# Inner products of a recommendation tower, copied from PSUM with samples innermost instead of columns innermost

## The chip, the core and the metric

The kernel runs on one core of a Trainium2 chip. A core has a matrix engine (TensorE, PE in the profile), three engines for elementwise work (VectorE is DVE, ScalarE is ACT, GpSimd is POOL), a queue engine for DMAs (SyncE, SP), an on-chip memory of 128 partitions (SBUF) and the matrix engine's output memory of 128 partitions by 8 banks of 512 float32 (PSUM). Each engine runs its own instructions in order and waits on semaphores for the others. The metric is the device time of one execution in microseconds, median over the runs shown; lower is better.

## The reference

512 samples, all in float32. Each sample has 26 rows of 64 numbers, looked up in tables, and 256 dense numbers. What is computed:

```python
x = layer_norm(dense_t @ Wd.T, gd, bd)                       # 512 x 128
y = layer_norm(einsum('bnd,ed->bne', sparse_t, Ws), gs, bs)  # 512 x 26 x 128
y = einsum('bne,pn->bep', y, Wsi)                            # 26 rows mixed into 32
y = swapaxes(layer_norm(y, gsi, bsi), 1, 2)                  # 512 x 32 x 128
T = concatenate([x[:, None, :], y], axis=1)                  # 512 x 33 x 128
Z = einsum('bnd,bmd->bnm', T, T)                             # inner products, 33 x 33 a sample
out = layer_norm(Z[:, TRIL_I, TRIL_J] @ Wl.T, gl, bl)        # 528 -> 512, the first 384 used
h = concatenate([out, dense], axis=1)
h = relu(h @ W_top1 + b_top1); h = relu(h @ W_top2 + b_top2); result = h @ W_top3
```

## The kernel before

**Tiles.** The 512 samples are 4 blocks of 128 (`BLOCKS`), a block is 4 units (`BU`), so there are 16 units of 32 samples (`UNITS`), each in two halves of 16. Unit `u` goes through these stages: `transposes` and `norms` on PE, `mult_a`, `sums_a`, `recip_a`, `scale_a` on DVE (the first layer norm, which scales the gathered rows `g_sb` in place), `mix` on PE (`psU`), `keep_u` on ACT (`U`), `project` on PE (`psB`, two halves), `add_b` on DVE (`B`), `squares_b` on ACT (`sqB`), `sums_b` on DVE (`ssB`), `deviation_b` on ACT (`sdB`), `recip_b` and `norm_b` on DVE (`T`), and `inner` on PE: 32 small matmuls, one per sample, the 32 mixed rows against all 33, into `psZ` (seen by the profile as 64 instructions, L333).

**The inner products in PSUM.** `inner(u)` puts the products into four quadrants of 32 partitions, `gq` 0 to 3, eight samples (`GQ`) to a quadrant, and one sample after the other: in a partition there stand 8 samples of 33 columns (`COLS`), 264 numbers without a gap. The last unit uses `psU` in place of `psZ`.

**The copies.** Every quadrant is copied into `Zs` in SBUF, on 32 partitions. There the order is columns first and samples last, 64 samples (`PS`) to a column, so that the neighbour of a number in the next column lies 64 float32 (256 bytes) away and that of the next sample beside it. `z_places(u, gq)` (L206) gives both access patterns. 61 copies are ACT's (`keep_z`, L639) and 3 are DVE's (L1073, for the last two units). `relay` (L212) then moves `Zs` by DMA into `Zt`, on other partitions: 7 DMAs for a block, or for half of the last block. `linear` (L352, L424) multiplies `Zt` by `wl_g`.

**Order.** The order on each engine is written out by hand in a function `step(t)` for every engine. On ACT, step `t` is: `keep_u(t)`, `rows_out(t + 1)` (`sT`), two `squares_b`, `enter_x`, `deviation_a(t + 1)` (`sdA`), then `keep_z(t - 1, 0)`, `deviation_b(t, 0)`, `keep_z(t - 1, 1)`, `keep_z(t - 1, 2)`, `deviation_b(t, 1)`, `keep_z(t - 1, 3)`, and some single instructions of other stages; then `keep_u(t + 1)` of the next step. On DVE it is: two `add_b`, `mult_a` and `sums_a` of the next unit, `sums_b(t, 0)`, `recip_a`, `scale_a`, `sums_b(t, 1)`, then both `recip_b` and `norm_b`. On PE it is: `mix(t)`, `transposes(t + 1)`, `project(t)`, `norms(t + 1)`, `inner(t - 1)` and a part of the linear layers of an earlier block (`linear`, `variance`, `layer1`, `layer2`), or in the first steps other preparation.

**Around the copies.** `inner(u)` waits for the four copies of the unit before (`Z_kept`), since the bank is one. The relays of a block wait for its 16 copies. At the end ACT copies four quadrants in a row and DVE three; when all are there (`Z_kept` 64), the last 7 relays go out on three queues, ACT takes the root of the third block's variance (`zsd`, L660), and the third and fourth block's last layers follow.

Of the kernel before, what the change touches and what calls it, by code (L numbers as in the profile page):

```python
# [13 lines left out]
E, PROJ = 128, 32  # L14
# [6 lines left out]
BLOCKS, BU, HS, US = 4, 4, 64, 16  # L21
# [9 lines left out]
COLS = PROJ + 1  # L31
# [15 lines left out]
GQ = 8  # L47
# [21 lines left out]
def tower(nc, table, ids, small, rows, bs_rows, dense, wl, w1, w2, out):  # L69
    with ExitStack() as ctx:  # L70
        def sb(name, shape, dt=F32):
            return ctx.enter_context(nc.sbuf_tensor(name, shape, dt))
# [74 lines left out]
        Zs = sb("Zs", [PROJ, 2, 2, 7 * CW, PS])  # L147
# [58 lines left out]
        def z_places(u, gq):  # L206
            b, lo = u // BU, 2 * US * (u % 2) + GQ * gq
            bank = psZ if u < UNITS - 1 else psU
            return (Zs[:, b % 2, u % BU // 2, 0:COLS, lo:lo + GQ].rearrange("p c s -> p s c"),
                    bank[gq * PROJ:(gq + 1) * PROJ, 0:GQ * COLS].rearrange("p (s c) -> p s c", s=GQ))  # L210

        def relay(queue, b, q, lo, hi, landed):  # L212

# [367 lines left out]
        def _(act):  # L581
# [48 lines left out]
            def keep_z(u, gq):  # L630
                b, j = u // BU, u % BU
                act.wait_ge(Z_done, 4 * u + gq + 1)
                if j == 0 and gq == 0:
                    if b == 0:
                        act.wait_ge(fills, 5)
                    if b >= 2:
                        act.wait_ge(d_zt[b - 2], 7 * 16)
                to, product = z_places(u, gq)
                act.activation(to, product, ACT.Copy).then_inc(Z_kept, 1)  # L639
# [157 lines left out]
        def _(dve):  # L797
# [272 lines left out]
            for u, gq in ((UNITS - 2, 3), (UNITS - 1, 2), (UNITS - 1, 3)):  # L1070
                dve.wait_ge(Z_done, 4 * u + gq + 1)
                to, product = z_places(u, gq)
                dve.tensor_copy(to, product).then_inc(Z_kept, 1)  # L1073
# [82 lines left out]
```

## Time and profile before

| What | Value |
|---|---|
| median of 3 runs | 186.32 us (186.28 to 187.85) |
| span of the profiled execution | 185.4 us |
| PE busy | 148.0 us (80%) |
| DVE busy | 130.1 us (70%) |
| ACT busy | 106.9 us (58%) |
| POOL busy | 104.3 us (56%) |
| copies of the inner products on ACT (L639) | 61, each about 0.616 us |
| copies of the inner products on DVE (L1073) | 3, each about 0.61 us |

A busy share is an average over the whole span and says nothing of who waits. The order of the steps does: from about 26 us to 164 us the kernel goes through 16 steps of 7 to 10 us, in each of which the four engines hand their work round. What a shorter instruction is worth is read from the wait that ends last in such a step.

### The profile page before, as it was taken

Reading aid. Unit: us, or ns where it says so; the run is one execution under the profiler, and the core shown is the slowest. Engines: PE = TensorE matmul, PEld = TensorE weight load, DVE = VectorE, ACT = ScalarE, POOL = GpSimd, SP = SyncE. Lnnn points to the kernel's source line nnn. Section 1 sums busy time; section 2 is a strip of 40 time slices with the busy share of each in tenths; the row PEclk is TensorE's granted clock in tenths of the full one; section 3 lists DMA queues with packets and bytes.
Section 4 is the critical chain, followed back from the end, with each engine's and each line's share of the span. In section 5 each row is a group of like instructions: output and inputs, shape, how many; then the busy total and the mean of one; then the engine's idle time right before and its main releaser. Section 6 shows DMA issues by size and latency. Waiting matters only on the chain.

```text
span 185.4 us, 4668 instructions
## 1 busy us (share of the span) xinstructions
PE 148.0 (80%) x1825; PEld 113.2 (61%) x1825; DVE 130.1 (70%) x300; ACT 106.9 (58%) x245; POOL 104.3 (56%) x111
## 2 busy tenths in 40 slices
PE   0089877977969947459996978899799799977995
PEld 0084544434549544419794947569596666877994
DVE  6269659772959594908697999579799967943142
ACT  1202435594868486866667877585877857831230
POOL 3778777877878777777777777777840000020000
PEclk9999999996999669855999999999999999997899
DMA  5816334141111112311111123111111100110000
GB/s 153 294 33 194 137 58 161 32 139 26 34 21 29 24 28 61 61 27 27 28 33 23 32 58 64 28 28 25 28 25 40 33 7 11 27 38 0 0 0 0
DMA packets 6003, 9.59 MB, mean 52 GB/s; under 512 B 2303, under 2 KB 3538, under 8 KB 5854
## 3 DMA queue, kind: packets, MB, share of 16 engines
q0 software_dynamic: 3392, 3.45, 10.3%
q1 hardware_dynamic: 2232, 5.08, 9.1%
q10 hardware_dynamic: 358, 0.78, 1.1%
q8 instruction: 14, 0.23, 0.5%
q14 instruction: 7, 0.06, 0.1%
HBM read 8.01 MB, written 0.00 MB: 43 GB/s over the span
## 4 chain that ended last, share of the span: by engine, by line
PE 40%; ACT 23%; DVE 19%; issue 11%; DMA 5%; ACTq 1%; DVEq 0%
PE psB L318 11%; ACT Zs L639 10%; DVE B L831 4%; ACT U L600 4%; DMA dense_sb<-in_dense 4%; PE psG L284 4%; DVE qA L809 4%; DVE prod L802 3%; PE psZ L333 3%; PE psW L352 3%; PE psU L299 3%; DVE ssB L838 3%; ACT sdB L617 2%; PE psB L520 2%; PE psZ L424 2%
## 5 line engine op out<-in xcount | busy, mean ns | idle before, releaser
L257 POOL DMA_INDIRECT g_sb<-in_table,row_id x104 | 102.8, 989 | 31.7 <-issue 31.4
L831 DVE TENSOR_TENSOR B<-psB,bias 128x512 f32<-128x512 f32 x31 | 20.0, 686 | 26.2 <-PE psB L318 26.2
L639 ACT ACTIVATE Zs<-psZ 32x264 f32<-32x264 f32 x59 | 36.3, 616 | 2.1 <-PE psZ L333 1.0
L318 PE MATMUL psB<-U,ws_g 64*128 64x512 f32 x64 | 20.9, 735 | 15.3 <-ACT U L600 15.2
L611 ACT ACTIVATE sqB<-B 128x512 f32<-128x512 f32 x31 | 19.1, 632 | 23.1 <-DVE B L831 23.1
L299 PE MATMUL psU<-wsi_x,g_sb 128*128 128x192 f32 (+4 forms) x128 | 23.3, 330 | 7.3 <-DVE g_sb L824 7.3
L299 PEld LDWEIGHTS psU<-wsi_x,g_sb 128*128 128x128 f32 x128 | 20.9, 206 | 11.1 <-DVE g_sb L824 11.0
L284 PEld LDWEIGHTS psG<-gram,sT 128*128 128x128 f32 x104 | 14.0, 207 | 14.5 <-ACT sT L587 10.0
L850 DVE TENSOR_TENSOR T<-B,rB 128x512 f32<-128x512 f32 x31 | 21.5, 692 | 1.1
L838 DVE TENSOR_REDUCE ssB<-sqB 128x16 f32<-128x512 f32 x32 | 21.7, 677 | 0.1
L284 PE MATMUL psG<-gram,sT 128*128 128x128 f32 x104 | 17.2, 308 | 0.7 <-ACT sT L587 0.7
L318 PEld LDWEIGHTS psB<-U,ws_g 64*128 64x128 f32 x64 | 5.4, 208 | 20.0 <-ACT U L600 20.0
L214 POOL DMA_DIRECT2D Zt<-Zs x2 | 1.1, 549 | 26.5 <-ACT Zs L639 26.5
L333 PE MATMUL psZ<-T 128*32 128x33 f32 x960 | 13.0, 202 | 0.3 <-issue 0.2
L333 PEld LDWEIGHTS psZ<-T 128*32 128x32 f32 x960 | 10.8, 112 | 3.3 <-issue 1.6
L352 PE MATMUL psW<-Zt,wl_g 127*128 127x128 f32 x100 | 12.8, 286 | 0.0
L352 PEld LDWEIGHTS psW<-Zt,wl_g 127*128 127x128 f32 x100 | 12.1, 199 | 0.5 <-issue 0.4
L600 ACT ACTIVATE U<-psU 128x512 f32<-128x512 f32 x16 | 9.5, 595 | 2.5 <-PE psU L299 2.2
L802 DVE TENSOR_TENSOR prod<-psG,g_sb 128x384 f32<-128x384 f32 (+1 forms) x16 | 9.3, 583 | 2.1 <-PE psG L284 2.1
L594 ACT ACTIVATE sdA<-qA,eps_c 128x6 f32<-128x6 f32 (+1 forms) x16 | 4.8, 300 | 9.5 <-DVE qA L812 9.0
L824 DVE TENSOR_TENSOR g_sb<-g_sb,rA 128x384 f32<-128x384 f32 (+1 forms) x16 | 9.5, 592 | 0.6
L809 DVE TENSOR_REDUCE qA<-prod 128x6 f32<-128x384 f32 (+1 forms) x16 | 9.4, 586 | 0.6
(159 smaller groups left out, 226.7 us busy)
## 6 DMA issues: line engine op xcount, KB each, us to landing
g_sb<-in_table,row_id POOLq DMA_INDIRECT x104, 2.5
wl_sb<-in_wl SPq DMA_DIRECT2D x1, 1280.0 KB, 6.0
w_sb<-in_w SPq DMA_DIRECT2D x2, 512.0 KB, 5.4
w_sb<-in_w SPq DMA_DIRECT2D x1, 768.0 KB, 4.5
small_sb<-in_small SPq DMA_DIRECT2D x1, 615.5 KB, 4.1
dense_sb<-in_dense ACTq DMA_DIRECT2D x1, 512.0 KB, 7.3
Zt<-Zs SPq DMA_DIRECT2D x3, 80.0 KB
Zt<-Zs SPq DMA_DIRECT2D x3, 70.0 KB
```

The source lines that it names most:

```text
L257: pool.indirect_dma_start(g_sb[:, k, h * DSP:(h + 1) * DSP], None, table, bass.IndirectOffsetOnAxis(row_id[:, 2 * k + h:2 * k + h + 1], 0) ...
L284: mm = pe.matmul(psG[:, n * P:(n + 1) * P], sT[:, u % 2, n * P:(n + 1) * P], gram[:, :], start=True, stop=True)
L299: mm = pe.matmul(psU[:, (lo - US * j) * PROJ:(hi - US * j) * PROJ], g_sb[:, SLOTS * b + c, :], wsi_x[:, c, lo - s0:hi - s0, :], start=(n = ...
L318: pe.matmul(psB[h][:, :], ws_g[h * DSP:(h + 1) * DSP, :], U[h * DSP:(h + 1) * DSP, u % 2, :], start=not (last and h == 0), stop=True).then ...
L333: mm = pe.matmul(bank[gq * PROJ:(gq + 1) * PROJ, n * COLS:(n + 1) * COLS], T[:, u % 2, h, s, 2:2 + PROJ], T[:, u % 2, h, s, 0:COLS], start ...
L352: mm = pe.matmul(bank[:, at * BS:(at + 1) * BS], wl_g[0:KL, jj, f * P:(f + 1) * P], Zt[0:KL, b, :, jj, :], start=(jj == 0), stop=(jj == CW ...
L600: act.activation(U[:, u % 2, :], psU[:, :], ACT.Copy).then_inc(U_ready, 1)
L611: act.activation(sqB[:, h, :], at, ACT.Square).then_inc(B_squared, 1)
L639: act.activation(to, product, ACT.Copy).then_inc(Z_kept, 1)
L831: dve.tensor_tensor(B[:, h, :].rearrange("p (s j) -> p s j", j=PROJ), psB[h][:, :].rearrange("p (s j) -> p s j", j=PROJ), bias[:, :].rearr ...
L838: dve.tensor_reduce(ssB[:, h, :], sqB[:, h, :].rearrange("p (s j) -> p s j", j=PROJ), AX, ALU.add).then_inc(B_summed, 1)
L850: dve.tensor_tensor(T[:, u % 2, h, :, 2:], at.rearrange("p (s j) -> p s j", j=PROJ), rB[:, h, :].rearrange("p (s o) -> p s o", o=1).broadc ...
```

## The change

One function gives the access patterns of all 64 copies. Before, both were walked with samples outside and columns inside: the read from PSUM was one run of 264 numbers, and the write into `Zs` went 256 bytes on for each number. After, both are walked with columns outside and samples inside: the write goes in runs of 8 numbers side by side (32 bytes), 33 of them, and the read goes 33 float32 (132 bytes) on for each number. The same numbers go to the same places. Nothing else differs: no instruction, wait or buffer is added, removed or moved.

```diff
--- before.py
+++ after.py
@@ -206,8 +206,8 @@
         def z_places(u, gq):
             b, lo = u // BU, 2 * US * (u % 2) + GQ * gq
             bank = psZ if u < UNITS - 1 else psU
-            return (Zs[:, b % 2, u % BU // 2, 0:COLS, lo:lo + GQ].rearrange("p c s -> p s c"),
-                    bank[gq * PROJ:(gq + 1) * PROJ, 0:GQ * COLS].rearrange("p (s c) -> p s c", s=GQ))
+            return (Zs[:, b % 2, u % BU // 2, 0:COLS, lo:lo + GQ],
+                    bank[gq * PROJ:(gq + 1) * PROJ, 0:GQ * COLS].rearrange("p (s c) -> p c s", s=GQ))
```

On ACT the second step with copies reads as follows; each row is a line of the kernel, what it writes and reads, and the shape (partitions, then the free dimensions from the outer to the inner).

```order
 L626 ACTIVATE T<-xT 128x32
 L594 ACTIVATE sdA<-qA,eps_c 128x6
-L639 ACTIVATE Zs<-psZ 32x8x33
-L617 ACTIVATE sdB<-ssB,eps_c 128x16
-L639 ACTIVATE Zs<-psZ 32x8x33 x2
-L617 ACTIVATE sdB<-ssB,eps_c 128x16
-L639 ACTIVATE Zs<-psZ 32x8x33
+L639 ACTIVATE Zs<-psZ 32x33x8
+L617 ACTIVATE sdB<-ssB,eps_c 128x16
+L639 ACTIVATE Zs<-psZ 32x33x8 x2
+L617 ACTIVATE sdB<-ssB,eps_c 128x16
+L639 ACTIVATE Zs<-psZ 32x33x8
 L749 ACTIVATE wl_g,wl_sum<-wl_sb 128x512 x3
```

The places and their neighbours are the same; only the shape of the copies has turned from 8 by 33 to 33 by 8. On DVE the three copies at the end turn in the same way, and PE's rows are the same throughout.

## Rows read from the trace of the kernel before

**Rows 1.** The page: PE's granted clock in 40 slices, and the chain's lines.

```profile
PEclk9999999996999669855999999999999999997899
...
PE psB L318 11%; ACT Zs L639 10%; DVE B L831 4%; ACT U L600 4%; DMA dense_sb<-in_dense 4%; PE psG L284 4%; DVE qA L809 4%; DVE prod L802 3%; PE psZ L333 3%; PE psW L352 3%; PE psU L299 3%; DVE ssB L838 3%; ACT sdB L617 2%; PE psB L520 2%; PE psZ L424 2%
```

**Rows 2.** The waits: engine, line, releaser; us in total, times, longest.

```profile
DVE B L831 <- PE psB L318: 26.2, 15, 4.3
...
ACT U L600 <- PE psU L299: 2.2, 3, 1.7
```

**Rows 3.** ACT by line and shape: count, us busy, mean ns, idle before.

```profile
L639 ACT ACTIVATE Zs<-psZ 32x264 f32<-32x264 f32 x59 | 36.3, 616 | 2.1 <-PE psZ L333 1.0
...
L626 ACT ACTIVATE T<-xT 128x32 f32<-128x32 f32 x16 | 4.0, 248 | 0.0
...
L783 ACT ACTIVATE z_sq<-psZ 128x256 f32<-128x256 f32 x1 | 0.4, 383 | 5.8 <-DVE zT L907 5.8
...
L684 ACT ACTIVATE wsT<-psT 128x128 f32<-128x128 f32 x1 | 0.3, 277 | 1.5 <-PE psT L516 1.5
```

**Rows 4.** DVE by line and shape: copies out of PSUM, and two memsets.

```profile
L1073 DVE COPY Zs<-psU 32x264 f32<-32x264 f32 x2 | 1.2, 612 | 0.1
...
L907 DVE COPY zT<-psZ 128x256 f32<-128x256 f32 x1 | 0.4, 424 | 5.7 <-PE psZ L424 5.7
...
L941 DVE MEMSET gram<- 128x128 f32 x1 | 0.2, 165 | 0.0
...
L938 DVE MEMSET T<- 128x64 f32 x1 | 0.1, 112 | 0.0
```

**Rows 5.** The timeline of step 8, all engines: start, length, engine, line.

```profile
104.00 0.68 DVE L838 TENSOR_REDUCE ssB<-sqB 128x16 f32<-128x512 f32 x1
...
104.33 0.60 ACT L639 ACTIVATE Zs<-psZ 32x264 f32<-32x264 f32 x1
...
104.75 0.28 ACT L617 ACTIVATE sdB<-ssB,eps_c 128x16 f32<-128x16 f32 x1
...
105.05 1.27 ACT L639 ACTIVATE Zs<-psZ 32x264 f32<-32x264 f32 x2
105.29 0.68 DVE L838 TENSOR_REDUCE ssB<-sqB 128x16 f32<-128x512 f32 x1
...
105.79 1.23 PE L299 MATMUL psU<-wsi_x,g_sb 128*128 128x128 f32 x8
...
106.13 0.26 ACT L617 ACTIVATE sdB<-ssB,eps_c 128x16 f32<-128x16 f32 x1
...
106.42 0.63 ACT L639 ACTIVATE Zs<-psZ 32x264 f32<-32x264 f32 x1
...
107.55 0.60 ACT L600 ACTIVATE U<-psU 128x512 f32<-128x512 f32 x1
```

**Rows 6.** The timeline of step 11, ACT and PE.

```profile
129.68 0.61 ACT L639 ACTIVATE Zs<-psZ 32x264 f32<-32x264 f32 x1 [0.28 <-PE psZ L333]
...
130.39 1.26 ACT L639 ACTIVATE Zs<-psZ 32x264 f32<-32x264 f32 x2
...
130.44 1.26 PE L299 MATMUL psU<-wsi_x,g_sb 128*128 128x160 f32 x8
...
132.65 0.59 ACT L600 ACTIVATE U<-psU 128x512 f32<-128x512 f32 x1
```

**Rows 7.** The timeline of ACT where it waits for PE.

```profile
90.04 0.60 ACT L600 ACTIVATE U<-psU 128x512 f32<-128x512 f32 x1 [0.16 <-PE psU L299]
```

**Rows 8.** The timeline where the last copies end.

```profile
162.18 1.25 DVE L1073 COPY Zs<-psU 32x264 f32<-32x264 f32 x2
162.23 1.26 ACT L639 ACTIVATE Zs<-psU 32x264 f32<-32x264 f32 x2
...
163.52 1.73 ACTq L214 DMA_DIRECT2D Zt<-Zs  x2
```

**Rows 9.** The timeline of PE, where it has waited for ACT.

```profile
81.41 2.08 PE L318 MATMUL psB<-U,ws_g 64*128 64x512 f32 x4 [2.12 <-ACT U L600]
```

## The prediction, made before the changed kernel ran

> **What bounds the kernel now.** I read the page first: the chain that ended last changes engines all the time, and no engine is its bound for long. Its second largest line is the one that the change touches, the copies on ACT, with 10% of the span [rows 1]. That is an upper limit, not a price: the chain names what an engine was doing, and something else may be nearly as late. The waits come next: DVE stands 26.2 us for the product `psB`, in 15 waits, while ACT stands only 2.2 us for `psU`, in 3 [rows 2]. So in most of the 16 steps the mixed rows in `psU` are there already when ACT takes them, and ACT is what is late. Last I read the timeline of single steps. A step turns round once from one `U` copy (L600) to the next: `U`, then PE's `psB`, DVE's `B` and its sums, ACT's roots and copies of inner products, and the next `U`.
>
> Step 8 is the common form [rows 5]. DVE's first `ssB` ends at 104.00 + 0.68 = 104.68 and ACT's first root `sdB` starts at 104.75, so it waits for DVE although a copy is in front of it. The second `ssB` ends at 105.29 + 0.68 = 105.97; the second `sdB` starts at 106.13, 0.16 us later. The last copy follows at 106.42, and `U` at 107.55. PE's `mix` had ended at 105.79 + 1.23 = 107.02, so PE would have allowed `U` at about 107.06 (where ACT waits for `mix`, it goes on about 0.04 us after the end).
>
> **What the change does to one copy.** Nothing is added or moved, so the whole matter is the length of 64 instructions. ACT's reads of PSUM that are contiguous and are written contiguously take 277 ns for 128 numbers and 383 for 256 [rows 3]: 106 ns for 128 more, 0.83 ns a number, and 171 ns fixed. The copy of 264 numbers ought to take 171 + 264 x 0.83 = 390 ns. It takes 616, which is (616 - 171) / 264 = 1.69 ns a number, twice as much. The writes that go on by 256 bytes are the only unusual thing in it, since it reads one run. ACT's small write into `T`, with 136 bytes from one number to the next, points the same way: 248 ns for 32 numbers, where the line gives 171 + 27 = 198 (its source is in SBUF, so a part of the 50 ns may be that). DVE shows it too: 612 ns for 264 numbers against 424 for 256 [rows 4]. One pair of rows speaks against it: the memset of 64 places at 136 bytes takes 112 ns, no more for each than the contiguous one of 128 in 165 [rows 4]. A memset reads nothing, so I give it little weight, and a pitch of 136 bytes isn't one of 256.
>
> After the change the write has runs of 8 and should cost what a contiguous one costs. The new cost is the read from PSUM at 132 bytes a number, and no row of this trace has one, on any engine. From below its cost is nothing: 390 ns for a copy on ACT. From above, the nearest row is the strided write itself, 616 ns: the two would then have changed places. A read that is worse than the write is not excluded by any row. I take 390, because what these rows show slow is a write into SBUF, and because a read whose next address is known ahead can be under way while others are finished, which is an argument and no row. That is the choice on which all else hangs.
>
> The Trainium skill ("Advanced Engine Details and Errata", PSUM Cachelines) says the opposite: PSUM works in lines of 8 bytes, so each two consecutive numbers should lie together, and its sentence on patterns with gaps is about matmuls. The same page's SBUF Cachelines (16 bytes, at least two accesses to a line for full rate) agrees with the 616 against 390 ns of the write. By the first rule the gain of the write is lost again in the read and the sum below would be about nothing; this is the second case further down.
>
> **What a step gains.** A copy shortens by 616 - 390 = 0.226 us. That isn't 4 x 0.226 = 0.90 for each of the 14 steps that have four copies, for DVE comes next.
>
> - Common step, by [rows 5]: the copy ahead of the first `sdB` gains nothing, since that root already waits for DVE. The two copies behind it would bring the second root 0.45 earlier, but DVE's `ssB` allows only 105.97 + 0.05 = 106.02, so 0.11. The fourth copy gains its full 0.226. Together 0.33 us, and `mix` allows 107.55 - 107.06 = 0.49, so it stands. Six steps read so (1, 2, 4, 5, 8, 13), with 0.30 to 0.33 each: 1.9 us.
> - Steps with a late first copy, by [rows 6]: in step 11 the copies wait behind `z_sq` and PE's products, until 129.68, when DVE's sums are done. Then all four gain, 0.90, and `mix` (130.44 + 1.26 = 131.70, `U` now at 132.65) allows 0.91. Steps 7, 9 and 11 are like it: 2.7 us.
> - Steps where `mix` is late. `U` at 90.04 waits for PE [rows 7]. Steps 3, 6 and 12 gain nothing, and steps 10 and 14 only up to `mix`, 0.18 and 0.09: 0.3 us.
> - The end, by [rows 8]: ACT's last copies, four without a pause, end at 162.23 + 1.26 = 163.49, and DVE's last two run from 162.18 to 163.43. ACT would gain 0.9. On DVE a contiguous copy of 264 would take 424 + 8 x 1.04 = 432 ns, 0.18 less than 612; its last two cannot start before PE's last products at about 162.1, so they end at about 163.0. The relays start when both are done, at 163.05 instead of 163.52, and ACT's next root stands behind its own two relays: 0.45 us.
>
> The sum is 1.9 + 2.7 + 0.3 + 0.45 = 5.3 us. The profiled execution has a span of 185.4 us, and the median of the runs is 186.3, 0.9 more for what lies around it. Span after: 180.1; time after: **181.0 us**. The 9 us of busy time that are set free on ACT and the 5.3 of the span are thus two numbers: the rest becomes idle time behind DVE's sums and PE's `mix`.
>
> What is late next: DVE's run from `B` to the second `ssB`, without a gap in it, and PE's linear layers ahead of `mix`. The DMA queues see the relays of a block come a little earlier, into stretches in which nobody waits for them.
>
> PE's clock is the uncertain part of this case. It is granted in full in most slices and falls to the lower level around 42 to 46, 60 to 70 and 76 to 87 us [rows 1], and before most of these falls PE had stood idle for some 2 us. At 81.41, behind 2.12 us of waiting for `U`, `psB` takes 2.08 us [rows 9] at the lower level, 1.2 GHz, half of the full 2.4, so about 1 us more. Shorter steps shorten such pauses by 0.3 us. I cost it at nothing, with one or two such losses either way, so this case has a range of its own of 178.5 to 183.
>
> **The other ways.**
>
> 1. The read costs part of it (copy of 450 to 560 ns). As the second root needs only 0.11 us, even a gain of 0.1 us a copy gives 0.2 in six common steps, 0.4 in three long ones and 0.3 in steps 10 and 14 together; with 0.2 at the end that is 2.9, so 183.4, in a band from 182 to 184.5.
> 2. It costs what the write did (the page's rule on 8-byte lines, at the price that [rows 3] show for 264 scattered numbers): each copy still takes 616, no step moves, and the time is **186.3**. For it: symmetry, and the twofold rate looks like one access in two cycles. Against it: it would have to be so in another memory.
> 3. Slower: the read costs more than the write. There is no cover against a longer copy, for it delays every ACT-bound step in full, four times. At three cycles, 2.5 ns a number, a copy takes 171 + 660 = 831 ns, 0.215 more; 0.86 x 12 steps, 0.4 and 0.7 in steps 3 and 6 beyond what ACT now waits, and 0.8 at the end make 12.2: **198.5**. At 2.5 cycles, 720 ns, it is 0.42 in each of 12 steps, 0.3 in the others and 0.4 at the end: 192. It decides against the change from 30 ns more a copy (0.03 x 4 x 14 = 1.7 us) on. For it: the read goes on by a new, odd pitch (33 numbers) each time, and nothing here bounds it. Against it: no row of ACT or DVE shows a number that costs more than about two of the contiguous ones.
> 4. The copies are short but the steps don't follow, since PE's clock falls once or twice more or DVE holds them: 184.5 to 187. The rows of step 11 leave only 0.01 us beside the full gain, so such a limit is near.
>
> **How the numbers follow.** My forecast has 0.57, case 1 0.08, case 2 0.13, case 3 0.17, case 4 0.05. A measurement of this kernel tells about 1%, 1.9 us, from no change. Faster by more than that: the forecast, case 1 and a small part of case 4, 0.66. Within 1%: case 2 and most of case 4, 0.17. Slower: case 3, 0.17. The range goes from 178 (0.04 left out below, where the clock would have to help) to 189 (most of case 3, some 0.15, left out above).
>
> **What the profile after would show.** The copies (L639) at about 390 ns and DVE's at about 430, if the read is free; at 616 and 612 if the costs changed places; above 650 if it is worse. In a common step the second `sdB` starts 0.05 us after the second `ssB` ends, and `U` comes 0.33 us earlier after the `U` before it, not 0.90. The steps 7, 9 and 11 shorten by 0.9. ACT's waits for DVE `ssB` and for PE `psU` grow; the relays of the end start about 0.5 us closer to the end of the last products. The forecast is wrong if the copies are short and the common step gains 0.1 or 0.9, if the clock falls in another place, or at its root if a number read from PSUM 132 bytes on costs more than one beside it.

## The result and the profile after

| | before | after |
|---|---|---|
| median of 5 runs | 186.28 us (185.39 to 187.85) | **177.3 us** (176.97 to 180.81) |
| ratio of the times, with its 95% interval | | **0.956** (0.951 to 0.961) |
| span of the profiled execution | 185.4 us | 179.0 us |
| mean granted TensorE clock in it | 0.936 | 0.943 |
| first `U` to the last relays' issue in it | 25.77 to 163.52 | 25.53 to 158.74 |

The change gave about 9 us in this comparison, where 5.3 were forecast. Here and below, a ratio sets against each other only the runs within 1.5% of a kernel's fastest in the same comparison, while a median takes them all. The profiled execution of after is one of those in which the clock fell most: the other four have spans of 175.2 to 176.1 us, so its steps are to be read against each other, and its span isn't the typical one.

How much of the 9 us is the clock can be bounded by laying runs of equal mean clock side by side, over all comparisons of this document (33 runs of the kernel before, 9 of the changed one). At 0.981 the spans are 180.0, 181.3 and 181.7 us before and 175.2 to 175.9 in four runs after, 5.5 us less on average; at 0.943 to 0.945 they are 183.9 (11 runs) and 179.6 (2 runs) on average, 4.3 less. The median clock is 0.944 before and 0.961 after. So 4.3 to 5.5 us come at an equal clock, near the forecast, and what goes beyond comes with a clock that falls less.

The page of after: the granted clock, the chain by engine and line, and three groups (busy, mean ns, idle before and what ended it). They answer to [rows 1] and [rows 3].

```profile
PEclk9999999997899657956999999999999999999999
...
PE 44%; DVE 25%; ACT 14%; issue 10%; DMA 5%; ACTq 1%; DVEq 0%
PE psB L318 11%; DVE ssB L838 7%; PE psG L284 6%; PE psW L352 5%; ACT U L600 5%; DMA dense_sb<-in_dense 4%; DVE B L831 4%; DVE qA L809 4%; DVE prod L802 3%; PE psU L299 3%; ACT Zs L639 3%; PE psZ L333 2%; DVE g_sb L824 2%; PE psB L520 2%; ACT wl_g L754 2%
...
L639 ACT ACTIVATE Zs<-psZ 32x264 f32<-32x264 f32 x59 | 22.4, 379 | 1.7 <-PE psZ L333 0.6
...
L617 ACT ACTIVATE sdB<-ssB,eps_c 128x16 f32<-128x16 f32 x32 | 9.7, 304 | 4.1 <-DVE ssB L838 4.0
L600 ACT ACTIVATE U<-psU 128x512 f32<-128x512 f32 x16 | 9.5, 595 | 3.0 <-PE psU L299 2.8
```

A copy on ACT takes 379 ns instead of 616. The copies' share of the chain went from 10% to 3%, and `ssB` on DVE, which had 3%, has 7%: what was ACT's is DVE's now. `sdB` waits 4.0 us for `ssB` in all, and the wait for `psU` grew from 2.2 to 2.8.

DVE's copies at the end, by line and shape in the profile after (612 ns in [rows 4]):

```profile
L1073 DVE COPY Zs<-psU 32x264 f32<-32x264 f32 x2 | 0.9, 430 | 0.2
```

Step 8 of after in the timeline (start, length, engine, line), to be laid beside [rows 5]:

```profile
102.23 0.36 ACT L639 ACTIVATE Zs<-psZ 32x264 f32<-32x264 f32 x1
...
102.61 0.31 ACT L617 ACTIVATE sdB<-ssB,eps_c 128x16 f32<-128x16 f32 x1
...
102.94 0.79 ACT L639 ACTIVATE Zs<-psZ 32x264 f32<-32x264 f32 x2
103.19 0.68 DVE L838 TENSOR_REDUCE ssB<-sqB 128x16 f32<-128x512 f32 x1
...
103.69 1.23 PE L299 MATMUL psU<-wsi_x,g_sb 128*128 128x128 f32 x8
...
103.90 0.31 ACT L617 ACTIVATE sdB<-ssB,eps_c 128x16 f32<-128x16 f32 x1 [0.16 <-DVE ssB L838]
104.23 0.39 ACT L639 ACTIVATE Zs<-psZ 32x264 f32<-32x264 f32 x1
...
105.25 0.60 ACT L600 ACTIVATE U<-psU 128x512 f32<-128x512 f32 x1
```

The first root comes 0.38 us behind the first copy's start, before 104.75 - 104.33 = 0.42, though the copy is 0.24 shorter: it waits for DVE, as before. The second root starts at 103.90, DVE's sum having ended at 103.19 + 0.68 = 103.87, with a wait of 0.16 us that wasn't there before. From the first copy to `U` it takes 3.02 us, before 107.55 - 104.33 = 3.22.

Step 11, to be laid beside [rows 6]:

```profile
126.39 0.38 ACT L639 ACTIVATE Zs<-psZ 32x264 f32<-32x264 f32 x1 [0.31 <-PE psZ L333]
...
126.99 0.79 ACT L639 ACTIVATE Zs<-psZ 32x264 f32<-32x264 f32 x2
...
128.68 0.59 ACT L600 ACTIVATE U<-psU 128x512 f32<-128x512 f32 x1
```

From the first copy to `U`: 2.29 us, before 132.65 - 129.68 = 2.97.

**From `U` to `U`, step by step.** All starts are rows of L600 in the two timelines; the last line is from the last `U` to the relays' issue on ACT. For the common steps the prediction has 0.30 to 0.33 each and the sum of 1.9; the column's split of it among them is made afterwards.

| step | before, us | after, us | gain | forecast |
|---|---|---|---|---|
| 1, 2 | 9.38, 10.32 | 9.07, 10.09 | 0.31, 0.23 | 0.33, 0.33 |
| 3 | 8.07 | 7.66 | 0.41 | 0 |
| 4 | 10.23 | 10.46 | -0.23 | 0.30 |
| 5, 6 | 9.95, 9.26 | 9.78, 8.81 | 0.17, 0.45 | 0.31, 0 |
| 7 | 9.71 | 9.17 | 0.54 | 0.90 |
| 8 | 7.80 | 7.61 | 0.19 | 0.33 |
| 9 | 8.38 | 7.53 | 0.85 | 0.90 |
| 10 | 7.50 | 7.34 | 0.16 | 0.18 |
| 11 | 9.22 | 8.56 | 0.66 | 0.90 |
| 12 | 7.40 | 7.41 | -0.01 | 0 |
| 13, 14 | 7.86, 7.49 | 7.55, 7.40 | 0.31, 0.09 | 0.31, 0.09 |
| the end, to the relays | 8.12 | 7.70 | 0.42 | 0.45 |

Together 4.55 us against 5.3. That leaves 6.4 - 4.55 = 1.85 us of the difference of the two spans outside the steps: 0.24 before the first `U`, and 1.6 behind the relays, where nothing was changed. That is the next reading.

The timeline of PE at the end, of before and then of after, with the idle time ahead in brackets:

```profile
168.12 1.18 PE L397 MATMUL psW<-h1T,w_sb 128*128 128x128 f32 x8 [2.30 <-ACT h1T L779]
169.12 2.33 PE L424 MATMUL psZ<-Zt,wl_g 127*128 127x128 f32 x10
171.24 1.68 PE L397 MATMUL psW<-h1T,w_sb 128*128 128x128 f32 x8
172.75 1.28 PE L424 MATMUL psZ<-Zt,wl_g 127*128 127x128 f32 x10
```

```profile
163.34 1.16 PE L397 MATMUL psW<-h1T,w_sb 128*128 128x128 f32 x8 [1.79 <-ACT h1T L779]
164.34 1.28 PE L424 MATMUL psZ<-Zt,wl_g 127*128 127x128 f32 x10
165.46 1.06 PE L397 MATMUL psW<-h1T,w_sb 128*128 128x128 f32 x8
166.35 1.28 PE L424 MATMUL psZ<-Zt,wl_g 127*128 127x128 f32 x10
```

The same ten matmuls take 2.33 us before and 1.28 after, the next eight 1.68 and 1.06. From the first row to the fourth it is 4.63 us before and 3.01 after, which is the whole 1.6. The windows of PE there (us, PE busy and count, granted clock, DMA share, GB/s), before and after:

```profile
170.00:172.00 2.00, 2.00 (x11) 0.50 0.00 0
```

```profile
166.00:168.00 2.00, 2.00 (x20) 1.00 0.00 0
```

The clock stood at the lower level, 1.2 GHz, behind a pause of 2.30 us, and at 2.4 GHz behind one of 1.79. So between these two profiles time was also gained where the change hadn't touched anything, through PE's clock. That the shorter pause is the reason is not shown: in a run further down PE pauses 2.26 us in the same place and keeps the higher level.

### The profile page after: what moved, and what is told of

The parts are those of the page before. It is cut to its first block, busy times and chain, and to the rows that moved or that the text cites. A ratio compares the mean times of both kernels' runs of the same rounds, so it can differ in the third digit from the quotient of the medians.

```text
span 179.0 us, 4668 instructions
## 1 busy us (share of the span) xinstructions
PE 145.6 (81%) x1825; PEld 110.5 (62%) x1825; DVE 129.8 (73%) x300; ACT 98.7 (55%) x245; POOL 103.5 (58%) x111
## 4 chain that ended last, share of the span: by engine, by line
PE 44%; DVE 25%; ACT 14%; issue 10%; DMA 5%; ACTq 1%; DVEq 0%
PE psB L318 11%; DVE ssB L838 7%; PE psG L284 6%; PE psW L352 5%; ACT U L600 5%; DMA dense_sb<-in_dense 4%; DVE B L831 4%; DVE qA L809 4%; DVE prod L802 3%; PE psU L299 3%; ACT Zs L639 3%; PE psZ L333 2%; DVE g_sb L824 2%; PE psB L520 2%; ACT wl_g L754 2%
## 5 line engine op out<-in xcount | busy, mean ns | idle before, releaser
L299 PE MATMUL psU<-wsi_x,g_sb 128*128 128x192 f32 (+4 forms) x128 | 22.6, 322 | 6.5 <-DVE g_sb L824 6.5
L299 PEld LDWEIGHTS psU<-wsi_x,g_sb 128*128 128x128 f32 x128 | 20.1, 200 | 10.6 <-DVE g_sb L824 9.6
L284 PEld LDWEIGHTS psG<-gram,sT 128*128 128x128 f32 x104 | 14.5, 213 | 14.5 <-ACT sT L587 10.0
L639 ACT ACTIVATE Zs<-psZ 32x264 f32<-32x264 f32 x59 | 22.4, 379 | 1.7 <-PE psZ L333 0.6
L284 PE MATMUL psG<-gram,sT 128*128 128x128 f32 x104 | 17.8, 315 | 0.7 <-ACT sT L587 0.7
L352 PE MATMUL psW<-Zt,wl_g 127*128 127x128 f32 x100 | 12.3, 278 | 0.0
L617 ACT ACTIVATE sdB<-ssB,eps_c 128x16 f32<-128x16 f32 x32 | 9.7, 304 | 4.1 <-DVE ssB L838 4.0
L352 PEld LDWEIGHTS psW<-Zt,wl_g 127*128 127x128 f32 x100 | 11.6, 192 | 0.5 <-issue 0.4
L600 ACT ACTIVATE U<-psU 128x512 f32<-128x512 f32 x16 | 9.5, 595 | 3.0 <-PE psU L299 2.8
```

What stands on the lines that cost most here:

```text
L284: mm = pe.matmul(psG[:, n * P:(n + 1) * P], sT[:, u % 2, n * P:(n + 1) * P], gram[:, :], start=True, stop=True)
L299: mm = pe.matmul(psU[:, (lo - US * j) * PROJ:(hi - US * j) * PROJ], g_sb[:, SLOTS * b + c, :], wsi_x[:, c, lo - s0:hi - s0, :], start=(n = ...
L352: mm = pe.matmul(bank[:, at * BS:(at + 1) * BS], wl_g[0:KL, jj, f * P:(f + 1) * P], Zt[0:KL, b, :, jj, :], start=(jj == 0), stop=(jj == CW ...
L600: act.activation(U[:, u % 2, :], psU[:, :], ACT.Copy).then_inc(U_ready, 1)
```

## The experiments

The questions were three: is the excess over the forecast the clock; is a copy's worth really set by what ends last behind it; and what exactly is it in the two access patterns that costs.

### The changed kernel again

No edit beyond the change itself.

> The changed kernel once more, to have it beside the others on one chip. Theory A (the gain is 5 to 6 us of shorter steps and the rest is PE's clock, which falls less often): ratio to before 0.950 to 0.965; where the profile has a mean granted clock of 0.98 the span is about 175.3, where it has 0.94 about 179. Theory B (the shorter copies explain all 9 us themselves): the span doesn't go with the clock.

178.14 us (177.53 to 181.96) against 185.87 of before in the same comparison (183.08 to 188.93), ratio 0.969 (0.958 to 0.980). The profiled span is 175.7 us at a clock of 0.981. The other profile of the same kernel has 179.0 at 0.943. Of the 3.3 us between them 0.7 lie ahead of the first `U` (25.53 and 24.82) and 2.6 behind it, in the steps whose clock differs. The span goes with the clock, as theory A says. The ratio missed its range of 0.950 to 0.965 by a little: before was itself anywhere between 183 and 189 in this comparison.

### Matmuls that only keep PE busy

Both kernels, each with the same additional lines. `eye_sb` is the identity; the results stand in banks that are written anew before anybody reads them.

```diff
+            def fill(to, n):
+                for _ in range(n):
+                    pe.matmul(to, eye_sb, eye_sb, start=True, stop=True)
...
             def mix(u):
                 b, j = u // BU, u % BU
+                if u in (5, 6):
+                    pe.wait_ge(U_ready, u)
+                    fill(psU[:, 0:P], 6)
                 pe.wait_ge(s_scaled, u + 1)
...
+                if u in (2, 3, 6):
+                    pe.wait_ge(B_added, 2 * u)
+                    fill(psB[0][:, 0:P], {2: 5, 3: 3, 6: 4}[u])
                 pe.wait_ge(U_ready, u + 1)
...
             third_layer1()
+            fill(psW[:, 0:P], 6)
             third_layer2(0, 2)
```

> The kernel before, with 30 matmuls of 128 columns more on PE, whose results nobody reads, where PE stood idle for 1.5 to 2.4 us: ahead of psB in steps 2, 3 and 6, ahead of mix in steps 5 and 6, and ahead of the first layer-2 product at the end. Theory A (the falls of the clock behind those pauses cost time): the granted clock goes from 0.936 to above 0.97 and the time falls by 3 to 6 us though work is added, to 181 to 183. Theory B (the clock costs nothing, since PE is not the bound there): the same time as before or up to 1 us more.

> The changed kernel with the same 30 matmuls. Theory A: the clock stands above 0.97 as in the same kernel of before, and the difference of the two is the gain of the copies alone, 4.5 to 5.5 us, so 176 to 177 here: little better than without them, since most falls are avoided already. Theory B: it is as much faster than the filled kernel of before as the changed one is than before, 8 to 9 us.

The kernel before went from 185.87 to 181.78 us (181.06 to 182.08) with work added; by the ratio it is 0.989 (0.982 to 0.996). The same kernel in the next comparison has 182.17 against 185.81 and a ratio of 0.994 (0.985 to 1.004). So the filled kernel is about 4 us faster than the typical run of before, and 0.6 to 1.1% faster than those of its runs in which the clock fell least. The changed kernel went from 178.14 to 177.47 (176.79 to 180.0), within its own spread. The granted clock on the pages of the filled kernel before, and of the changed kernel of the first experiment, unfilled:

```profile
PEclk9999999999998799999999999999999999999999
```

```profile
PEclk9999999999999997896999999999999999999999
```

Its lower slices around 42 to 46, 60 to 70, 76 to 87 and 165 to 175 us [rows 1] have shrunk to two mild ones, and the mean clock rose from 0.936 to 0.99. The page of the filled changed kernel has the same clock row as the unfilled one, so the additional matmuls did nothing for its clock. With the clock nearly the same (0.990 and 0.980 in the profiles) the two filled kernels differ by 181.78 - 177.47 = 4.3 us; without the one run of 180.0 us the changed kernel's median is 177.13 and the difference 4.65. Theory A had 4.5 to 5.5 for it. So theory A is shown for the sign and the order: 4.3 to 4.65 us are the copies', and the rest of the difference of 7.7 in this comparison, about 3, is time that the kernel before lost to the clock and the changed one mostly doesn't. Its size depends on which runs of before are taken (its medians lie at 185.8 to 186.3, single runs at 181.8 to 189.8; by the ratio of 0.969 the difference is 5.8 us, of which 1.2 to 1.5 are left for it), so I hold it at 1 to 4 us. That it is the shorter pauses which keep the clock up in the changed kernel is argued and not shown: the filled kernel before has pauses of 2.69 us (ahead of 68.57) and 2.31 us (ahead of 78.50) and keeps the full clock behind both.

### One copy at a time

On the filled kernel before, since its clock is steadier, the new patterns for some quadrants alone:

```diff
         def z_places(u, gq):
             b, lo = u // BU, 2 * US * (u % 2) + GQ * gq
             bank = psZ if u < UNITS - 1 else psU
+            if gq == 0:
+                return (Zs[:, b % 2, u % BU // 2, 0:COLS, lo:lo + GQ],
+                        bank[gq * PROJ:(gq + 1) * PROJ, 0:GQ * COLS].rearrange("p (s c) -> p c s", s=GQ))
+            return (Zs[:, b % 2, u % BU // 2, 0:COLS, lo:lo + GQ].rearrange("p c s -> p s c"),
+                    bank[gq * PROJ:(gq + 1) * PROJ, 0:GQ * COLS].rearrange("p (s c) -> p s c", s=GQ))
```

The other two have `gq in (1, 2)` and `gq == 3` for the condition.

> The kernel before with the 30 additional matmuls again, as the base for the next three, since its clock hardly falls. 181 to 182.5 by both theories.

> As the base, but the copy of quadrant 0 alone walks samples innermost (16 of 64 copies). Theory A (what a shorter copy is worth hangs on what ends last behind it: DVE's sum ends the wait behind the first copy in common steps): gain only in steps 7, 9 and 11, 0.2 us each, 0.3 to 0.8 us in all against the base. Theory B (each copy is worth its share of the whole, a quarter of 4.8 us): 1.2 us.

> As the base, but the copies of quadrants 1 and 2 alone turned (32 of 64). Theory A: 0.11 in six common steps, 0.45 in three long ones, something at the end, 2.0 to 2.5 us. Theory B: half of 4.8, 2.4 us; this run alone tells the two little apart, the three together do.

> As the base, but the copy of quadrant 3 alone turned (16 of 64, 2 of them on DVE). Theory A: nothing stands between the fourth copy and the next U, so it gains 0.2 us in nine steps, 0.2 in steps 10 and 14, and some 0.3 at the end: 2.0 to 2.5 us, four times the first copy's. Theory B: 1.2 us, the same as the first copy's.

| turned | copies | median, us | gain on the base |
|---|---|---|---|
| none | 0 | 182.17 (10 runs, 180.52 to 183.24) | |
| quadrant 0 | 16 | 181.71 (10 runs, 181.17 to 182.4) | 0.46 |
| quadrants 1, 2 | 32 | 180.19 (179.34 to 180.54) | 1.98 |
| quadrant 3 | 16 | 179.82 (178.81 to 180.42) | 2.35 |
| all, from the experiment above | 64 | 177.47 | 4.70 |

The first copies and the fourth are the same instruction 16 times, and each group became 0.24 us shorter a copy. The first gives 0.46 us, the fourth 2.35. The three gains add up to 4.79; all together gave 4.70 on this base, and 4.31 on that of their own comparison, whose median was 181.78. So the base alone moves by 0.4 us. Theory B, by which each is worth its share, asked 1.2 for both and is refuted. The gain of quadrant 0 is as large as the noise of these medians; that it is far below that of quadrant 3 is not in doubt (181.17 to 182.4 against 178.81 to 180.42). The middle two's 1.98 is just under the 2.0 to 2.5 expected.

The timelines show it without that noise, in two common steps, from `U` to `U` in us:

| step | none | quadrant 0 | quadrants 1, 2 | quadrant 3 | all |
|---|---|---|---|---|---|
| 1 | 9.38 | 9.39 | 9.31 | 9.13 | 9.07 |
| 13 | 7.85 | 7.86 | 7.79 | 7.69 | 7.55 |

The first copy is worth nothing there, the middle two 0.06 to 0.07 us, the fourth 0.16 to 0.25, all together 0.30 to 0.31. One part of the expectation for quadrant 3 failed: it had some 0.3 us for the end, and from the last `U` to the relays it takes 8.21 us against 8.11 in the base. ACT's last four copies are none of quadrant 3 and end at 158.32, the relays go out at 158.35.

### DVE's three copies as before

```diff
+            if u < UNITS - 2 or (u, gq) not in ((UNITS - 2, 3), (UNITS - 1, 2), (UNITS - 1, 3)):
```

The two branches are those of the experiment before.

> The changed kernel, but DVE's three copies at the end walk columns innermost as before. The end then waits for DVE's copies: the last relays start 0.4 us later, so the time is 0.3 to 0.5 us above the changed kernel's. If the wait there ends on ACT, no difference.

The times (181.09, from 177.81 to 182.67) can't tell 0.4 us, since in these runs the clock fell more than in most: 0.943 in the profile. But the timeline can. In it ACT's last copies and the relays on ACT's queue stand so:

```profile
158.04 0.79 ACT L642 ACTIVATE Zs<-psU 32x264 f32<-32x264 f32 x2
...
159.75 1.73 ACTq L217 DMA_DIRECT2D Zt<-Zs  x2
```

From the last `U` (151.59) it is 8.16 us to the relays, against 7.70 in the changed kernel and 8.12 in the one before: ACT's copies end at 158.83, and the relays start only 0.9 us later, when DVE's are done. With the long copies on DVE, the four short ones on ACT give nothing there. So the end's 0.45 needs DVE's three copies, and by the run with quadrant 3 alone it needs ACT's as well: each engine by itself holds it.

The same run bears on the clock. PE waits 2.26 us for `h1T` here, against 2.30 in the kernel before, and the ten matmuls behind it run at full speed:

```profile
164.36 1.16 PE L400 MATMUL psW<-h1T,w_sb 128*128 128x128 f32 x8 [2.26 <-ACT h1T L782]
165.36 1.28 PE L427 MATMUL psZ<-Zt,wl_g 127*128 127x128 f32 x10
```

So the length of that one pause doesn't decide whether the clock falls behind it; what does stays open.

### The price of an access pattern

To the end of the changed kernel, 15 copies on ACT and the same 15 on DVE, one after the other, from a PSUM bank that nobody writes any more:

```diff
+            act.activation(ra[0:32, 0:264], psB[1][0:32, 0:264], ACT.Copy).then_inc(r_act, 1)
+            act.wait_ge(r_act, 1)
+            act.activation(ra[0:32, 0:264].rearrange("p (c s) -> p c s", s=8), psB[1][0:32, 0:264].rearrange("p (s c) -> p c s", s=8), ACT.Copy).then_inc(r_act, 1)
...
+            act.activation(ra[0:32, 0:528].rearrange("p (n w) -> p n w", w=2)[:, :, 0], psB[1][0:32, 0:264], ACT.Copy).then_inc(r_act, 1)
...
```

Their lines on ACT: L799 contiguous; L801 and L803 read PSUM at 33 and 64 words; L809 writes at 64 words; L811 reads at 33 and writes at 64; L813, L815, L817 write at 2, 4 and 8 words; L819, L821 write pairs, 8 words from pair to pair, on even and on odd words; L823 is contiguous from SBUF, L825 and L827 read SBUF at 8 and 33 words.

> The changed kernel with 15 further copies at the end of ACT and 15 at the end of DVE, one at a time on 32 partitions, whose results nobody reads; only their lengths matter. Theory A (PSUM takes any pitch at full rate, the write into SBUF pays for each number that has no neighbour beside it): contiguous 390 ns on ACT and 430 on DVE; read at 33 and at 64 words the same; write at 64 words 616 and 612; both strided no more than the write alone; writes in pairs as contiguous; writes at 2 words already slow. Theory B (only the pitch of 256 bytes is slow, a matter of powers of two): writes at 4 or 8 words as contiguous, the read at 64 words slower than that at 33. A read from SBUF at 8 words: slow under A as the write is, or free if only writes pay.

ACT by line and shape (the mean of one is the second number behind the bar):

```profile
L825 ACT ACTIVATE w_sb<-wl_g 32x264 f32<-32x264 f32 x1 | 0.7, 672 | 0.0
L827 ACT ACTIVATE w_sb<-wl_g 32x264 f32<-32x264 f32 x1 | 0.7, 662 | 0.0
L817 ACT ACTIVATE w_sb<-psB 32x264 f32<-32x264 f32 x1 | 0.6, 636 | 0.0
L815 ACT ACTIVATE w_sb<-psB 32x264 f32<-32x264 f32 x1 | 0.6, 628 | 0.0
L811 ACT ACTIVATE w_sb<-psB 32x264 f32<-32x264 f32 x1 | 0.6, 607 | 0.0
L809 ACT ACTIVATE w_sb<-psB 32x264 f32<-32x264 f32 x1 | 0.6, 604 | 0.0
L823 ACT ACTIVATE w_sb<-wl_g 32x264 f32<-32x264 f32 x1 | 0.4, 425 | 0.0
L821 ACT ACTIVATE w_sb<-psB 32x264 f32<-32x264 f32 x1 | 0.4, 400 | 0.0
L819 ACT ACTIVATE w_sb<-psB 32x264 f32<-32x264 f32 x1 | 0.4, 397 | 0.0
L813 ACT ACTIVATE w_sb<-psB 32x264 f32<-32x264 f32 x1 | 0.4, 393 | 0.0
L801 ACT ACTIVATE w_sb<-psB 32x264 f32<-32x264 f32 x1 | 0.4, 380 | 0.0
L803 ACT ACTIVATE w_sb<-psB 32x264 f32<-32x264 f32 x1 | 0.4, 380 | 0.0
...
L799 ACT ACTIVATE w_sb<-psB 32x264 f32<-32x264 f32 x1 | 0.4, 366 | 0.0
```

DVE, seven of its rows: a write at 4 words (L1127), a read of SBUF at 33 words (L1139), a write at 2 words (L1125), reads of PSUM at 33 and 64 words (L1113, L1115), a read of SBUF at 8 words (L1137) and a contiguous one (L1135). Each pattern ran once on each engine.

```profile
L1127 DVE COPY wl_sb<-psB 32x264 f32<-32x264 f32 x1 | 0.6, 615 | 0.0
...
L1139 DVE COPY wl_sb<-wl_g 32x264 f32<-32x264 f32 x1 | 0.6, 599 | 0.0
...
L1125 DVE COPY wl_sb<-psB 32x264 f32<-32x264 f32 x1 | 0.4, 421 | 0.0
L1113 DVE COPY wl_sb<-psB 32x264 f32<-32x264 f32 x1 | 0.4, 420 | 0.0
L1115 DVE COPY wl_sb<-psB 32x264 f32<-32x264 f32 x1 | 0.4, 420 | 0.0
...
L1137 DVE COPY wl_sb<-wl_g 32x264 f32<-32x264 f32 x1 | 0.4, 384 | 0.0
L1135 DVE COPY wl_sb<-wl_g 32x264 f32<-32x264 f32 x1 | 0.3, 284 | 0.0
```

Theory A stands for PSUM: read at 33 or 64 words, ACT takes 380 ns and DVE 420, 14 and 11 ns more than contiguous (366 and 409). Theory B falls: a write at 4 or 8 words is as slow (628, 636) as one at 64 (604), so no power of two is behind it, and the read at 64 words isn't slower than that at 33. One point of theory A was wrong: a write at 2 words is not slow (393 ns). For a write the next number needn't lie right beside the last: 8 bytes on it is nearly free, 16 bytes on it is paid (a pitch of 12 bytes, and a pair across a 16-byte boundary, weren't run). And SBUF charges the reader too: ACT takes 672 and 662 ns for reads with a pitch of 8 and 33 words, against 425. DVE's reads of SBUF don't follow one such rule: at 33 words it takes 599 ns, at 8 words 384, contiguous 284. Why 8 words cost DVE so much less than 33 stays open. The prices of the strided write do not rise further where the read has a pitch as well (607).

The Trainium skill ("Advanced Engine Details and Errata", SBUF Cachelines) speaks of lines of 16 bytes and two accesses to each; the rows of writes at 2 and at 4 words agree, and DVE's read at 8 words, 384 ns where the one at 33 words takes 599, isn't explained by it. Its PSUM Cachelines, read as a rule for all engines, would have left the copy at 616 ns; by the rows of L801 and L803 it doesn't hold for a read by ACT, and by L1113 and L1115 not for one by DVE.

### Runs of two

```diff
-            return (Zs[:, b % 2, u % BU // 2, 0:COLS, lo:lo + GQ],
-                    bank[gq * PROJ:(gq + 1) * PROJ, 0:GQ * COLS].rearrange("p (s c) -> p c s", s=GQ))
+            return (Zs[:, b % 2, u % BU // 2, 0:COLS, lo:lo + GQ].rearrange("p c (r s) -> p r c s", s=2),
+                    bank[gq * PROJ:(gq + 1) * PROJ, 0:GQ * COLS].rearrange("p (r s c) -> p r c s", s=2, c=COLS))
```

> The changed kernel with copies that write runs of two numbers, not of eight: four passes over the 33 columns, the read still 33 words on within a pair. If a neighbour within 16 bytes is all that the write needs, as the separate copies with pairs had it (397 ns on ACT), the copies take 380 to 400 ns and the time is that of the changed kernel, 177 to 178. If the length of the run matters, between that and the kernel before.

In the kernel the 59 copies take 390 ns on average with runs of two, 379 with runs of eight:

```profile
L639 ACT ACTIVATE Zs<-psZ 32x264 f32<-32x264 f32 x59 | 23.0, 390 | 1.7 <-PE psZ L333 0.6
```

So a neighbour is enough, as expected. The time doesn't say it: 180.14 us (178.7 to 183.68), 2 to 3 above the changed kernel, where 11 ns a copy can't make more than 0.7 (0.011 x 64). The profiled one has 176.9 us of span at a clock of 0.971; from the first to the last `U` it needs 124.4 us, against 122.9 in the first experiment, and steps 5 and 6 alone, at the lower clock, make 11.11 + 8.87 against 10.37 + 8.18, which is 1.43 of the 1.44. Whether the clock falls more often in this kernel than in the changed one (0.971, 0.952, 0.961 and 0.944 in four runs), or did so by chance, stays open; the expected 177 to 178 us was missed.

### The fourth copy ahead of the root

Common steps now end on a root that waits 0.16 us for DVE. The copy behind it doesn't need that root:

```diff
                     keep_z(t - 1, 1)
                     keep_z(t - 1, 2)
-                    deviation_b(t, 1)
                     keep_z(t - 1, 3)
+                    deviation_b(t, 1)
```

> The changed kernel with ACT's fourth copy moved ahead of the second root sdB, so that the copy fills the 0.16 us for which that root waits for DVE in the changed kernel. If that wait is what common steps now end on, U comes 0.15 to 0.2 us earlier in about 8 steps and nothing is lost, since the later root delays only DVE's second norm, behind which DVE has 1 us to spare: 1.0 to 1.5 us less than the changed kernel, which had 177.3 and 178.1, if the clock doesn't fall more often. If PE's mix or DVE's norm is as late as the root, no gain.

> The same with the 30 additional matmuls: 176.0 to 176.8 against 177.5 without the move, and the same 177.5 if the wait wasn't the end of the step.

176.98 us (176.7 to 180.68) and with the added matmuls 176.74 (176.38 to 178.62). Against 177.3 and 178.14 without the move it is 0.3 to 1.2 us less, and 0.7 less on the filled kernels; both comparisons are inside the spread, so it is no worse and perhaps a little better; 1.0 to 1.5 us were expected. It is more interesting where the gain went. `U` of step 10 starts at 106.57 (first `U` at 24.90), against 109.52 (24.82) in the first experiment: 3 us ahead. Half of that, 0.73 + 0.85, is from steps 5 and 6, over which the clock differs between the two profiles, so it can't all be put down to the move; steps 1, 2, 4, 8 and 9 have 0.20 to 0.33 each. `U` of step 12 starts at 124.76 against 125.40: 0.6 ahead. In between, the timeline of PE reads:

```profile
106.88 0.33 PE L273 MATMUL psT<-small_sb,g_sb 128*128 128x128 f32 x1 [0.39 <-DMA g_sb<-in_table,row_id]
...
116.62 0.33 PE L273 MATMUL psT<-small_sb,g_sb 128*128 128x128 f32 x1 [1.68 <-DMA g_sb<-in_table,row_id]
```

PE waits for gathered rows. POOL issues 104 gathers one after the other, one each 1.25 us:

```profile
112.55 0.94 POOL L257 DMA_INDIRECT g_sb<-in_table,row_id  x1 [0.30 <-issue]
113.80 0.94 POOL L257 DMA_INDIRECT g_sb<-in_table,row_id  x1 [0.31 <-issue]
```

The last goes out at 136.8 us here and between 135.4 and 137.2 in the other profiles that bear on this, the kernel before (136.3) among them, whatever the other engines do. A block of four units needs 26 of them, 32.5 us, and the four steps 8 to 11 of the changed kernel already take less, 128.68 - 97.64 = 31.0 us in its first profile, living on a lead that the gathers had won in the longer steps before. Move steps closer still, and the lead is used up. That is the next bound: what shortens steps further is waited away in front of `transposes`.

## Why the prediction was right, and where it fell short

**The copy: right.** 379 ns on ACT and 430 on DVE against 390 and 432. That the strided write was the cost was read from rows, with a base line from two contiguous reads. The price of the strided read was a choice between two ends, and the low end was the true one. The memset whose places lay 136 bytes apart had spoken against the write's cost; no run explains it, and giving it little weight was right, since a copy's write at 16 or 32 bytes is as slow as one at 256.

**The common step: right in its mechanism, a little large.** The first copy gains nothing, DVE's `ssB` caps the middle two, the fourth gains. The experiments with single quadrants show it directly: 0.46, 1.98 and 2.35 us in all, and in step 13 nothing, 0.06 and 0.16. But the fourth copy's gain was put at 0.226 us throughout, and in step 8 it was 0.14: where an instruction with its source in SBUF stands behind it, it used to start 0.20 us before the long copy's end (106.85 against 106.42 + 0.63) and now starts 0.10 before the short one's (104.52 against 104.23 + 0.39). The same shows in steps 7 and 11, of the steps with a late first copy: from the first copy's start to the root behind it 0.43 and 0.42 us became 0.29 in both, 0.14 and 0.13 less where the copy is 0.24 shorter. They gained 0.54 and 0.66 us for 0.90 each. Step 9 gained 0.85 in another way than forecast: its first copy had waited 0.43 us for `psZ` and no longer does, so the step took the common form (its second root now waits 0.17 us for DVE), and quadrant 3 alone brings 0.64 of it (8.23 to 7.59). The term of the three, 2.7 us, was mis-sized by 0.65.

**PE's `mix` as a cap: right** in steps 10, 12 and 14 (0.16, -0.01, 0.09). Steps 3, 4 and 6 went their own way (0.41, -0.23, 0.45 for 0, 0.30, 0), and the mean clock over them was another in the two profiles: 0.96 and 1.00, 0.70 and 0.51, 0.65 and 0.79. On the filled kernels, too, step 3 gained something, 7.73 to 7.57, where nothing was forecast.

**The end: right**, 0.42 for 0.45, and for the reason given: the relays start when both engines are done, and in the changed kernel it is DVE whose three copies end last.

**The clock: the step that failed.** "I cost it at nothing, with one or two such losses either way" put a term at nothing in a kernel that had many such falls. The runs show it at 1 to 4 us in favour of the change, 1.6 us of them to be seen in one place at the end of the two profiles. Why the clock falls less in the changed kernel stays open: filling pauses with matmuls raised it in the kernel before, which speaks for the shorter pauses, and the pauses of 2.26 to 2.69 us without a fall behind them speak against so simple a rule. With the steps' 4.6 us measured for 5.3, the sum of the two errors takes the median to 177.3, 0.7 below the low end of the range, 178.0; the measured steps alone would have given 186.3 - 4.6 = 181.7. The direction, the mechanism and DVE's sums as what is late next were forecast, POOL's gathers as a bound were not; the size of 5.3 us was 60% of what was measured. That the time lies below the range, on the good side, is the clock's doing and no merit of the forecast.

**The span and the time.** The prediction put the time 0.9 us above the span. In every run whose span is on record it lies 1.8 above (180.81 and 179.0 for the profiled one), so the profiled execution of before, with its 185.4, was about 0.9 us longer than the median one. The forecast of 181.0 doesn't hang on it, since 5.3 from the median gives the same.

**The rivals.** Case 1 (the read costs a part), case 2 (the costs change places) and case 3 (the read costs more) fell with the length of the copies, case 4 (the clock falls more) with the clock's sign.

## What to carry to other kernels

A copy from PSUM that has to turn two dimensions should put the gaps into the PSUM read and the neighbours into the SBUF write: with at least two numbers to 16 bytes on the SBUF side it took 379 to 400 ns for 264 numbers here, without them 604 to 636. What the shorter instruction is then worth is read from the instruction that follows it on its engine and from what that one waits for: of three groups of the same copy, the first was worth a fifth of the last by the medians and nothing in the common steps. Where the granted clock of the matrix engine falls in the profile before, give it a term of its own in the sum, and compare kernels at an equal mean clock before their difference is put down to the change. Here that alone split 9 us into 4.3 to 5.5 and the rest.

## What the runs showed of the hardware that was not expected

- A read of PSUM at a pitch of 2, 33 or 64 words cost ACT and DVE at most 14 ns in 264 numbers. A read of SBUF at 8 or 33 words cost ACT 247 and 237 ns, DVE 100 and 315.
- A write into SBUF at a pitch of 2 words cost 27 ns on ACT, at 4 words 262. Read and write both with gaps cost no more than the write alone (607 and 604).
- Thirty matmuls whose results nobody reads made the kernel before about 4 us faster by the medians (185.87 to 181.78, and 185.81 to 182.17 again), its clock going from 0.936 to 0.99 in the profiles. By the ratios it is 0.989 and 0.994, the second with an interval that holds 1.
- The first `U` of the same instructions starts anywhere from 23.7 to 25.9 us in these profiles; comparisons of less than 2 us had to be made from a row within the kernel, not from its start.
